# A two-layer scan kernel on one core: TensorE's constant products at the head of layer 2 in blocks of 32 and 64 columns, and B's rows of two chunks written to diagonals in DRAM

## The reference

```python
# layer 1: bidirectional WKV over the tokens, with a receptance gate, a layer norm and an output product
x = x + _L0_conv_ref(_gn(x), ...)
# layer 2: bidirectional selective scan (Mamba), 384 inner channels, 16 states
x1 = _layernorm(tok, g1, b1);  x2 = _layernorm(tok, g2, b2)
x = x1 @ W_in_x.T;  z = x2 @ W_in_z.T
# per direction (_branch):
xc = silu(conv_b + sum(xp[:, k:k + L, :] * conv_w[:, k] for k in range(4)))
dbl = xc @ W_xproj.T
dt = softplus(dbl[..., :12] @ W_dt.T + dt_bias);  Bc, Cc = dbl[..., 12:28], dbl[..., 28:]
h = h * exp(dt_t * A) + (dt_t * x_t) * B_t;  y_t = sum_n h * C_t;  y = y + x * D
# both directions
out = ((y_f + y_b) * silu(z)) @ W_out.T + b_out
```

## Time and profile before

| | us |
|---|---|
| median of 3 runs | 19461.44 |
| lowest and highest run | 19454.89, 19484.83 |
| span of the profiled execution, its own time | 19481.1 |
| PE busy | 17354.2 (89%) |
| DVE busy | 17262.7 (89%) |
| POOL busy | 16894.1 (87%) |
| ACT busy | 13466.7 (69%) |
| DMA, hardware queue: share of 16 engines | 31.0% |

### The profile page before, as it was taken

The page is one execution under the profiler, slowest core; times in us unless marked ns, Lnnn a source line. Parts: engine busy times, 40 slices in busy tenths (PEclk is TensorE's granted clock), DMA queues, the critical chain, the costliest instruction groups (busy, mean ns, idle before and its releaser), DMA issues. The chain is left out here.

```text
span 19481.1 us, 179917 instructions
## 1 busy us (share of the span) xinstructions
PE 17354.2 (89%) x43808; PEld 7662.4 (39%) x43808; DVE 17262.7 (89%) x13583; ACT 13466.7 (69%) x33829; POOL 16894.1 (87%) x11028
## 2 busy tenths in 40 slices
PE   8989989899898898988989889898998989989898
PEld 3433434334343343433434334343343434434334
DVE  7988989889898898988989899898998989989899
ACT  6767767677676776767767677676776767767676
POOL 6979979799797997979979799797997979979799
PEclk9999999999999999999999999999999999999999
DMA  2313323233231332313323233232332323323233
GB/s 88 139 67 135 140 77 138 68 135 140 78 138 68 135 140 78 138 68 133 140 78 138 68 135 138 80 137 72 139 130 80 140 79 135 123 80 140 81 138 121
DMA packets 531163, 2179.01 MB, mean 112 GB/s; under 512 B 96586, under 2 KB 243684, under 8 KB 529956
## 3 DMA queue, kind: packets, MB, share of 16 engines
q1 hardware_dynamic: 529956, 2166.00, 31.0%
HBM read 1905.48 MB, written 245.63 MB: 110 GB/s over the span
## 5 line engine op out<-in xcount | busy, mean ns | idle before, releaser
L1133 DVE TENSOR_TENSOR_SCAN arena<-ps,arena 128x897 f32<-128x897 f32 x5376 | 10934.7, 2064 | 769.9 <-ACT arena L1287 477.1
L1339 POOL TENSOR_TENSOR arena<-arena 128x896 f32<-128x896 f32 x5376 | 9415.1, 1766 | 625.4 <-PE ps L1041 462.9
L1041 PE MATMUL ps<-arena,ident 128*128 128x448 f32 x21504 | 8997.4, 557 | 892.1 <-POOL arena L1339 889.4
L1271 ACT ACTIVATE ps<-arena,A 128x448 f32<-128x448 f32 x10752 | 6384.6, 626 | 1996.8 <-DVE arena L1133 1963.7
L1041 PEld LDWEIGHTS ps<-arena,ident 128*128 128x128 f32 x21504 | 4039.4, 193 | 5509.2 <-issue 3680.2
L1331 POOL TENSOR_TENSOR arena<-arena 128x896 f32<-128x896 f32 x2688 | 4762.4, 1772 | 84.2 <-DMA arena<-bc_rows 84.2
L1122 DVE TENSOR_TENSOR arena<-ps,arena 128x896 f32<-128x896 f32 x2688 | 2864.3, 1066 | 56.0 <-DMA arena<-bc_rows 56.0
L996 PE MATMUL ps<-arena,diag 128*128 128x448 f32 x5248 | 2087.8, 540 | 2.2
L996 PEld LDWEIGHTS ps<-arena,diag 128*128 128x128 f32 x5248 | 985.9, 189 | 1014.3 <-issue 943.4
L1320 POOL TENSOR_TENSOR arena<-arena 128x448 f32<-128x448 f32 x672 | 653.3, 979 | 512.7 <-DVE arena L1102 512.7
L1035 PE MATMUL ps<-arena,skipd 128*128 128x448 f32 x1344 | 715.9, 616 | 387.2 <-DVE arena L1109 265.6
(11 more groups left out here) (170 smaller groups left out, 19045.8 us busy)
## 6 DMA issues: line engine op xcount, KB each, us to landing
arena<-bc_rows SPq DMA_DIRECT2D x1776, 896.0 KB, 4.6
x_projected<-arena SPq DMA_DIRECT2D x112, 672.0 KB, 3.5
y_forward<-arena SPq DMA_DIRECT2D x112, 672.0 KB, 3.5
arena<-x_projected SPq DMA_DIRECT2D x112, 672.0 KB, 5.7
arena<-y_forward SPq DMA_DIRECT2D x112, 672.0 KB, 4.0
x<-in_x SPq DMA_DIRECT2D x119, 336.0 KB, 3.6
x_normed<-arena SPq DMA_DIRECT2D x112, 336.0 KB, 2.8
arena<-x_normed SPq DMA_DIRECT2D x112, 336.0 KB, 4.6
```

Source lines behind the costliest of these rows:

```text
L1041: m = e.matmul(y, ident[:, :], pr[:, q % NPR, a * T:a * T + T], start=False, stop=p == NP - 1 and a == 1)
L1133: e.tensor_tensor_scan(rev(hh[:, q % NH, 0:W2], s), rev(decays(q)[:, 0:W2], s), rev(bb[:, q % NB, 0:W2], s), car[:, k, n:n + 1] if i % NC ...
L1271: e.activation(two(decays(q))[:, a, :], dt[:, r % NDT, :], ACT.Exp, scale=Am[s][:, k, 2 * p + a:2 * p + a + 1]).then_inc(c_ex, 1)
L1339: e.tensor_tensor(pr[:, q % NPR, :].rearrange("p (a b) -> p a b", a=2), two(hh[:, q % NH, :]), cr[:, 2 * p:2 * p + 2, :], ALU.mult).then_i ...
```

## The change

It has three parts.

1. `busy_tiles` is new and takes the place of `busy(e, 2, DUBANK)` at the head of layer 2. It issues 8 products of 32 weight columns by 448 moving columns, 8 of 64 by 224, 8 of 64 by 112, and 8 of 32 by 224, each group as blocks that write neighbouring partitions (four blocks of 32 or two of 64 fill a bank), with 128 or 112 rows of constants, and then 4 transposes of 112 columns of `skipd`. Nobody reads the results. All other calls of `busy` stay.
2. SP's "cw" of chunks 3 and 9 issues a second DMA, after the store of B and C: the 16 rows of B (in chunk 9 the first 4), each value to a place of its own on the diagonal of a 112 x 112 block in a new DRAM tensor `zd`. Nobody reads `zd`.
3. A new semaphore `s_zd` counts these DMAs. ACT's "p1" waits for the first before it overwrites `res` in chunk 4 (`i > 3`) and for the second in chunk 10 (`i > 9`), and SP waits for both at the end of the image. The semaphore is cleared with the others.

```diff
+    zd = nc.dram_tensor("b_diagonals", (NS, T // 112, 112, 112), F32, kind="Internal").ap()
...
+    def busy_tiles(e, b):
+
+        rhs = skipd[:, :, :, :].rearrange("p a b c -> p (a b c)")
+        for rows, m, n, rounds in ((128, 32, T, 2), (112, 64, T // 2, 4), (112, 64, T // 4, 4), (112, 32, T // 2, 2)):
+            for k in range(rounds):
+                for j in range(128 // m):
+                    o = m * k % 128
+                    e.matmul(ps[m * j:m * j + m, b, 0:n], ident[0:rows, o:o + m], rhs[0:rows, 0:n],
+                             start=True, stop=True)
+        for k in range(4):
+            e.transpose(ps[0:112, b, 0:128], rhs[:, 112 * k:112 * k + 112], ident[:, :])
...
-    s_bf = sem("b_first")
+    s_bf, s_zd = sem("b_first"), sem("b_scattered")
...
         n1.tensor(e, w, 0)
-        busy(e, 2, DUBANK)
+        busy_tiles(e, DUBANK)
...
                         w.wait_ge(s_cw, 16 * i)
+                        if i > 3:
+                            w.wait_ge(s_zd, 16)
+                        if i > 9:
+                            w.wait_ge(s_zd, 32)
...
                 e.dma_start(cd[i % 2], res[32:64, :]).then_inc(s_cw, 16)
+                if i in (3, 9):
+                    n = NS if i == 3 else 4
+                    with nc.allow_non_contiguous_dma(reason="one value per row of a block"):
+                        e.dma_start(zd[0:n].rearrange("n k a b -> n k (a b)")[:, :, 0:112 * 112:113],
+                                    res[32:32 + n, :].rearrange("p (k a) -> p k a", a=112)).then_inc(s_zd, 16)
...
         w.wait_ge(s_dg, 32)
+        w.wait_ge(s_zd, 32)
```

More of the change, by code:

```diff
@@ L900, in build @@
              c_nq, c_nr, c_nm, c_pad, c_xh, c_c1, c_c2, c_c3, c_c4, c_t1, c_t2, c_t3, c_du,
-             c_dp, c_z1, c_z2, c_z3, c_z4, c_g, s_nw, s_xw, s_yw, s_cw, s_dg, s_out, *s_xl, *s_nl, *s_yl, s_bf, *s_bl, *s_cl]
+             c_dp, c_z1, c_z2, c_z3, c_z4, c_g, s_nw, s_xw, s_yw, s_cw, s_dg, s_out, *s_xl, *s_nl, *s_yl, s_bf, s_zd, *s_bl, *s_cl]
     def filled(w, name, i, e=0):
```

## The result

| | before | after |
|---|---|---|
| median of 6 runs, us | 19471.43 | 19534.06 |
| lowest and highest | 19454.89, 19487.77 | 19524.80, 19541.11 |
| span of the profiled execution | 19481.1 | 19534.8 |

The ratio is 1.0030, with a 95% interval from 1.0019 to 1.0041: slower, by 62.6 us between the medians and 53.7 us between the two profiled executions. The forecast was 19533. That is closer than its working deserves, and the closeness is luck: three more runs of before moved its median up by 10 us, and the change cost 63 us, not 72.

The account below looks back on a forecast made before the run. It took the single thread of waits at the start of layer 2 as the bound: blocks delaying L970 +72 us, scatters 0, added to the median 19461.4 for 19533 us. Range 19480 to 19625.

Parts of the forecast that it names:

- 4 transposes: Last group at layer 2's head: 8 records, 0.86 us by columns, at most 2.0 us; taken as 1.0 us.
- The blocks' length: PE at layer 2's head: the new groups take 6.2 us, L970 starts 4.5 us later, 72 us in 16 images.
- single-column pairs at the low clock: L719 and L720, 0.10 us apart at clock 0.50: weight loads may limit the 64 x 112 group to 0.84 us.
- Changes of block width: PE between groups at the head: 0.10 and 0.15 us seen per change, four changes taken as 0.5 us.
- lower bound of 56 us: Blocks at the head: 5.2 us of PE work by columns only, no changes of width, +3.5 us an image.
- My estimate from that figure: 32-column groups at the head, by the 2.38 speedup: 3.8 us instead of 2.34, whole change 23 us more.
- The scatters: Added DMAs, chunks 3 and 9: SP held 5.6 us, landing 13.8 us (bounds 7.2 to 41), hidden by 0.4, cost 0.
- The waits at "p1": ACT in chunks 4 and 10: new waits come some 70 us later, cost nothing unless the transfer takes that long.
- 1: Blocks at the head don't overlap as assumed: two at a time 19570, one at a time +214 us, 19675; chance 0.14.
- 2: Scatter in chunks 3 and 9 outlasts its slack: 20 us landing gives about 19720, 41 us gives 20370; chance 0.07.
- 3: Image lengths: the shift favours short images, at best 10 us slower, 19471, and up to 19500; chance 0.12.
- 4: PE after 18476: denser work keeps the clock up, some 5 us an image; at 8 us 19405; chance 0.03.

Follow-up runs that it names:

- plain products of equal length: Against the kernel before: 8 plain products of 384 columns and one of 192 at the head, no blocks or scatters; 19529.6 against 19469.3 us, ratio 1.0030.
- blocks only: The changed kernel without the two DMAs to diagonals and their waits, blocks at the head kept; 19526.8 us against 19469.3 before, ratio 1.0027.
- Scatters only: The changed kernel with the two plain products of 384 columns back at the head, both DMAs kept; 19466.1 us against 19469.3 before, ratio 0.9997.
- three scatters: The kernel before, plain products at the head, plus each of the two DMAs to diagonals issued three times in a row; 19976.6 against 19470.6 us, ratio 1.0262.
- two scatters: The kernel before, plain products at the head, plus each of the two DMAs to diagonals issued twice; 19689.5 against 19475.1 us, ratio 1.0110.
- The blocks spread over gaps: The changed kernel with each group of blocks in another gap of the head, replacing plain products there; 19478.2 us against 19470.6 before, ratio 1.0005.
- All together: The kernel before plus spread blocks, both scatters, fillers in two later gaps of the head and small products in backward chunks; 19581.6 against 19475.1 us, ratio 1.0056.

## Why the prediction was right

**What bounds.** Right: the head is one thread and L970's delay goes through to the end. The plain products of equal length show it without blocks (60.3 us for 59.7 of delay), and blocks only give 57.5 for 58.9.

**The blocks' length.** Forecast 6.2 us, measured 5.45 from L630's start to L983's. Term by term, by the records' starts in the last image:

| | forecast | to the next group's start |
|---|---|---|
| 8 of 32 x 448 | 1.5 | 1.64 |
| 8 of 64 x 224 | 1.5 | 1.56 |
| 8 of 64 x 112 | 0.84 | 0.87 |
| 8 of 32 x 224 | 0.84 | 0.89 |
| 4 transposes | 1.0 | 0.49 |
| changes of width | 0.5 | in the above, some 0.4 |
| sum | 6.2 | 5.45 |

The products run at the columns' pace, with four blocks of 32 at once or two of 64: 0.375 us for a round of records of 448 columns, 0.19 for 224, 0.095 for 112. The bound I took from the single-column pairs at the low clock didn't hold at the high one. The transposes were mis-sized: I counted two records each, as for a product; they have one, 0.11 us apart, so the term was double. With "Changes of block width" the sum comes out 0.75 us too long. Another 0.1 us is a slip in reading: L620 began at 18449.74, not at "about 18449.9", and the blocks begin 0.26 us behind the norm's second sum, which would be 18449.80 there. The delay was 3.68 us and not 4.5, 58.9 us and not 72. The mechanism was right, and the transposes are the term that was off most. The lower bound of 56 us held, but not by its working: my own terms by columns alone give 5.36 us, not 5.2, and with the transposes counted once 4.93.

Weighing the Trainium skill: "TensorE: Matmul & The Clock Gate", Part 3, gives a speedup of 2.38 for three blocks. My estimate from that figure made the 32-wide groups 3.8 us; they took 1.64 + 0.89 = 2.5 with a change of width in each. Here four blocks gave four times the pace, so the estimate was wrong for this case; no run here has three blocks. On the drain at a change of mode, in the Trainium skill's "TensorEngine Tiling (Array Packing)", "Key Properties", the trace agrees: a group whose width differs from the next one's takes 0.12 to 0.15 us more than its columns, and the group of 64 x 224, which the other 64-wide group follows, 0.06.

**The scatters.** Hidden, as forecast, and in good part by luck, since the working was off in all its parts and two errors offset each other. SP is held 5.9 us, near my 5.6, yet on the next DMA and not on the scatter (0.66 us). The values are through after 8.8 us, nearer to my lower bound of 7.2 than to 13.8: 5 us too long in the sum. The load behind needs longer than I gave it: it lands 5.8 us after the scatter is through, not 3.0, so 2.8 us too short. The difference is the slack, 2.6 us instead of 0.4. In the profile of "Scatters only" the slack was 0.1 to 0.7 us, so the 0 us that I took stood on little. The stretch from chunk 2 to 3 lasts 69.98 us before and after, and the next one 70.12. The issue of the first B load behind the second scatter, with a quarter of the values, took 5.80 us, as long as behind the first. The Trainium skill's "DMA: Bandwidth & Descriptors", "How many engines (k)", lets one expect that, with four engines for 4 rows, and the trace agrees: while the values pass, the DMA share of the 16 engines is 0.13 for the second scatter and 0.64 for the first.

**The waits at "p1".** In the whole profile "p1" (L1231) waits for PE's L1016 alone, as forecast.

**Rivals.** 1: refuted in the trace, and its serial form is now measured, 232 us (193 to 253) where I had 214. 2: not in the changed kernel; its mechanism is shown by two and three scatters. I put its price at 6 us twice an image for a landing of 20 us; two scatters (20 to 22 us) cost 9.0 + 1.8 in chunk 3 and some 2 around chunk 9. 3: between the profiles of before and after the deal of long and short images went neither way, which is luck too. The image lengths lie between 1214.8 and 1223.8 us after, 1211.3 and 1222.0 before, and the mean moved from 1214.8 to 1218.6, 3.8 us, close to the 3.68 of the head. But the rival is no idle one: the profiled execution of the plain products, with the same delay, had only images of the short kind and was 48 us under its kernel's median, and an execution of before took 19432.3 us, 37 us under its median. 4: the clock can be kept up there, and it brings next to nothing.

**Left open.** Why some images are 4 to 10 us longer than others was argued from low-clock stretches and not shown. It can separate two executions of one kernel by as much as the whole change costs: that of plain products had one of 19481.9 us and others of up to 19543.6. Open is also why a single scatter took 8.3 to 9.3 us in one profile and up to 11.3 in another.

## What to carry to other kernels

Filler work for an engine is free up to the length of the gap in which it stands, and costs its excess in full where the gap lies on a single thread; before adding some, read the gap from the timeline ("idle before"), and split the work over several gaps if it doesn't fit. For a DMA put in front of others, what counts is when the transfers behind it land against their readers, not the DMA's own issue time. Read that margin in every image and in more than one execution: here it was 2.6 us in one place and 0.1 in another, for the same code. A second such DMA had no slack left to use and cost nearly its whole length, where the first cost nothing.

## What the runs showed of the hardware that I had not expected

- Four products with 32 weight columns each, written to neighbouring partitions, run at once without loss: 16 records of 448 columns in 1.64 us, one change of width included. Written to the same partitions the 64 records of all groups take 14.05 us instead of 5.04.
- An f32 transpose of 112 columns is one record, and four follow each other at 0.11 us.
- A DMA of 7168 single values issues in 0.66 us, the next DMA's issue takes 5.9 us, and the last value is through 8.3 to 9.3 us after the issue in the changed kernel's profile. It took 9.9 to 11.3 us in "Scatters only", 9.1 to 10.4 in "The blocks spread over gaps" and 9.3 to 10.8 in "All together". Two in a row take 20.3 to 22.3 us and three 31.2 to 33.6. From first value to last that is 1.1 to 1.5 ns a value alone and 1.4 to 1.5 in a row, so that a row costs more than in proportion is not shown beyond the spread of single ones.
- 1792 values in 4 rows hold the queue almost as long as 7168 in 16 rows: 5.80 and 5.87 us for the issue of the load behind, and the last value through after 7.4 us in all four profiles with one scatter.
- PE's granted clock could be held at 1.00 over 24 us that had 0.64, for a gain too small to measure.
